# Wavelet convolution, batch norms and median blur on one core: the first stage's work is divided anew between POOL, VectorE and TensorE

## The chip, the cores and the metric

The kernel runs on one NeuronCore of a Trainium2 chip. The metric is the device time of one execution in microseconds. Data are float32 throughout; only the matmuls that do nothing but keep TensorE busy are bf16.

## What is computed

The input x has 16 images of 128 channels and 32 x 32 pixels. Cut to what matters:

```
a1, h1, v1, d1 = dwt2(x)                      # one Haar step over rows and columns: four 16x16 bands
proc(c)  = relu(batchnorm(einsum(c, conv_w)) * gamma + beta)   # 1x1 conv, statistics over all images
rimg0    = idwt2(proc(a1), proc(h1), proc(v1), proc(d1))
rimg1    = x                                   # three dwt steps and their inverses give x back
y        = conv3x3(concat([rimg0, rimg1]), convW_w) + convW_b
y        = relu(batchnorm(y))                  # statistics over all images again
out      = y + conv1x1(median3x3(y), W) + b
```

Both batch norms need a statistic over all 16 images before any image can go on. That divides the kernel into a first stage (split, 1x1 conv, bands, statistics), a long middle (3x3 conv and the medians of its output), and an end.

## The kernel before

Channels lie on the 128 partitions. All engines run programs written out by hand, in program order, and wait on semaphores. Nothing but these orders sets the order of the work.

**First stage, image by image.** SP's queue loads image n into one of eight ring buffers (`ring`; the program's names for them are raw, ru03, ru12 and xu03). `make_xu12` (L201, L202) adds and subtracts the even and odd columns and writes them to the image's slot in y. VectorE does this for the images in `BY_DVE` = (0, 5, 10) with `split_x`, POOL for the other 13. TensorE multiplies by w1 into one_ps, which has room for two images (`through_w1`, L332; four rows of the trace for an image, since an f32 matmul shows twice). ScalarE copies the odd rows out (`keep_odd`, L448), and VectorE adds and subtracts even and odd rows into the four bands in z (`bands`, L595 and L596). The product of image n+2 waits for the bands of image n. Then statistics: VectorE takes three bands with `band_stats` (L602), for two images at once, and `image_stats` (L607) for the last two images; ScalarE sums the fourth band and its squares.

**The taps.** The 3x3 conv is computed in a form that works on sums and differences of columns. For it the three column taps are mixed once: outer sum, middle plus outer, middle minus outer (`mix_taps`, L614 to L618, on VectorE behind the bands of image 2), and one half of them is halved by ScalarE (L472, L473).

**Early products.** The 3x3 conv works in units: an image, or half of one for images 0, 1, 14 and 15. The products of x for the first two units, `pq_of_x`, 12 of them, do not need the statistics. TensorE does them between the w1 products of images 5 to 13, as many behind each as `FILLS` says (L350, conv_ps<-y).

**After the statistics.** VectorE aggregates (L640), a short chain of tiny operations gives scale and shift, ScalarE normalises the bands of images 0 and 1 (`norm_bands`, L484), VectorE makes the row sums and differences of each (`make_ru12`, L208 and L209), and TensorE starts `pq_of_r` for units 0 and 1, four groups of three products, and then `outputs(0)`. POOL makes two more planes for every image (`make_xu03`, L269 and L271; `make_ru03`, L284 to L292). From then on VectorE alternates between `seed` (L688, L689) and the median network (L710 to L763).

**TensorE's clock.** `WARM_UP` matmuls on zeros stand at the start of the program (L393), and `KEEP_WARM` ones (L428) before the last stage.

Of the kernel before, what the change touches and what calls it, by code (L numbers as in the profile page):

```python
# [5 lines left out]
def wavelet_conv_median_kernel(nc, x, w1_t, w3_t, w2_t, vectors, out):  # L6
# [14 lines left out]
    PIX = H * W  # L21
# [14 lines left out]
    WARM_UP, KEEP_WARM = 8, 24  # L36
# [27 lines left out]
    with ctx:  # L64
# [75 lines left out]
        dve_done = sem("dve_done")  # L140
        taps_mixed = sem("taps_mixed")
# [5 lines left out]
        bands_normed = sem("bands_normed")  # L147
        ru12_made = sem("ru12_made")
# [99 lines left out]
        def _(pool):  # L248
# [6 lines left out]
            for n in BY_POOL:  # L255
                pool.wait_ge(x_in[n % RING], 16 * (n // RING + 1))
                make_xu12(G, n).then_inc(xu12_by_pool, 1)

# [64 lines left out]
        def _(pe):  # L323
# [71 lines left out]
            early = [(u, b, ky) for u in range(2) for b in range(2) for ky in KY_ORDER]  # L395
# [6 lines left out]
            assert not early  # L402
# [35 lines left out]
        def _(act):  # L438
# [28 lines left out]
            for n in range(IMAGES):  # L467
                keep_odd(n)
                if n == 3:
# [11 lines left out]
            def norm_bands(n):  # L481
                for b in range(BANDS):
                    band = zslot(n)[:, b * BAND:(b + 1) * BAND]
                    ins = S.activation(band, band, ACT.Relu, bias=bn1[:, 5, b:b + 1], scale=bn1[:, 4, b:b + 1])  # L484
                ins.then_inc(bands_normed, 1)
# [82 lines left out]
        def _(dve):  # L568
# [29 lines left out]
            def band_stats(p):  # L598
                dve.wait_ge(bands_made, 2 * p + 2)
                two = z[:, 2 * p:2 * p + 2, :].rearrange("c a q -> c (a q)")  # L600
                for b in range(DIAG):
                    step(V.bn_stats(stats1[:, b, p, :], at(two, b * BAND, [[PIX, 2], [1, BAND]])))  # L602
# [6 lines left out]
            def mix_taps():  # L609
                dve.wait_ge(w3_in, 16)  # L610
                row = [[KX * CH, 2 * KY], [1, CH]]
                left, mid, right = (at(wt[:, :], kx * CH, row) for kx in range(KX))
                dense = [[CH, 2 * KY], [1, CH]]
                step(V.tensor_tensor(at(outer_taps, 0, dense), left, right, ALU.add))  # L614
                after()
                step(V.tensor_tensor(at(v1[:, :], 0, dense), mid, at(outer_taps, 0, dense), ALU.add))
                after()
                V.tensor_tensor(mid, mid, at(outer_taps, 0, dense), ALU.subtract).then_inc(taps_mixed, 1)  # L618

            split_x(0)  # L620
            for n in range(IMAGES):
                bands(n)
                if n == 2:
                    mix_taps()
                if n == 3:
# [47 lines left out]

            for t in (col_lo, col_mid, col_hi):
                step(V.memset(at(t, 0, [[PITCH, H + 1]]), LOW))

            for n in range(2):
                dve.wait_ge(bands_normed, n + 1)
                wait_xu12(dve, RING + 5 - n)
                make_ru12(V, n).then_inc(ru12_made, 1)  # L680
# [209 lines left out]
```

## Time and profile before

| | before |
|---|---|
| median of 3 runs | 449.26 us (449.07 to 454.04) |
| profiled execution | 449.9 us, its span 447.8 us |
| TensorE busy | 403.3 us, 90% |
| VectorE busy | 408.8 us, 91% |
| ScalarE busy | 149.1 us, 33% |
| POOL busy | 197.9 us, 44% |
| mean granted TensorE clock | 0.96 of full speed |

Times in the trace count from the span's start. Two engines are busy nine tenths of the span, so shares alone do not tell which is waited for; the rows below are read from single stretches. The granted clock is given as a share of full speed: 1.00 is 2.4 GHz, 0.50 is 1.2 GHz.

### The profile page before, as it was taken

Reading aid. Unit: us, or ns where it says so; the run is one execution under the profiler, and the core shown is the slowest. Engines: PE = TensorE matmul, PEld = TensorE weight load, DVE = VectorE, ACT = ScalarE, POOL = GpSimd, SP = SyncE. Lnnn points to the kernel's source line nnn. Section 1 sums busy time; section 2 is a strip of 40 time slices with the busy share of each in tenths; the row PEclk is TensorE's granted clock in tenths of the full one; section 3 lists DMA queues with packets and bytes.
Section 4 is the critical chain, followed back from the end, with each engine's and each line's share of the span. In section 5 each row is a group of like instructions: output and inputs, shape, how many; then the busy total and the mean of one; then the engine's idle time right before and its main releaser. Section 6 shows DMA issues by size and latency. Waiting matters only on the chain.

```text
span 447.8 us, 3637 instructions
## 1 busy us (share of the span) xinstructions
PE 403.3 (90%) x1119; PEld 214.6 (48%) x1120; DVE 408.8 (91%) x535; ACT 149.1 (33%) x342; POOL 197.9 (44%) x186
## 2 busy tenths in 40 slices
PE   7497809999999999999999999999999986858896
PEld 2143408885544444444444444444446675743332
DVE  2978874799987999999999999999999999999996
ACT  2333663341413132223313132223313321216922
POOL 5996009080628182644627182644628510003730
PEclk9978967999999999999999999999999998969999
DMA  8960020010011010101011010101010000000557
GB/s 315 405 240 1 2 94 0 0 49 0 10 40 47 0 48 0 48 0 47 8 40 48 0 47 0 48 0 47 9 39 1 0 1 1 0 0 0 228 242 282
DMA packets 7651, 26.70 MB, mean 60 GB/s; under 512 B 976, under 2 KB 1232, under 8 KB 7504
## 3 DMA queue, kind: packets, MB, share of 16 engines
q1 hardware_dynamic: 7632, 26.48, 15.6%
q8 instruction: 8, 0.13, 0.1%
q14 instruction: 11, 0.09, 0.1%
HBM read 18.09 MB, written 8.39 MB: 59 GB/s over the span
## 4 chain that ended last, share of the span: by engine, by line
DVE 69%; PE 25%; issue 3%; ACT 1%; DMA 1%; POOL 0%; DVEq 0%; SPq 0%
PE conv_ps L350 19%; PE one_ps L332 5%; DVE one_ps L711 4%; DVE sorted_cols L747 4%; DVE one_ps L759 4%; DVE one_ps L761 4%; DVE sorted_cols L755 4%; DVE z L763 3%; DVE one_ps L745 3%; DVE sorted_cols L716 3%; DVE sorted_cols L714 3%; DVE sorted_cols L718 3%; DVE sorted_cols L713 3%; DVE sorted_cols L757 3%; DVE sorted_cols L753 3%; DVE y L841 3%
## 5 line engine op out<-in xcount | busy, mean ns | idle before, releaser
L350 PE MATMUL conv_ps<-ru,wt 128*128 128x512 f32 (+1 forms) x360 | 133.6, 508 | 0.0
L350 PE MATMUL conv_ps<-xu,wt 128*128 128x496 f32 (+3 forms) x240 | 89.9, 512 | 11.5 <-DVE conv_ps L689 11.5
L350 PEld LDWEIGHTS conv_ps<-ru,wt 128*128 128x128 f32 x360 | 70.5, 196 | 53.7 <-issue 49.7
L518 ACT ACTIVATE y<-conv_ps,sgn 128x512 f32<-128x512 f32 (+1 forms) x40 | 25.5, 639 | 185.1 <-PE conv_ps L350 185.1
L269 POOL TENSOR_TENSOR xu<-raw 128x480 f32<-128x480 f32 x16 | 17.2, 1072 | 139.5 <-PE conv_ps L350 139.4
L350 PEld LDWEIGHTS conv_ps<-xu,wt 128*128 128x128 f32 x240 | 46.6, 195 | 48.2 <-issue 33.2
L350 PE MATMUL conv_ps<-ru,v 128*128 128x496 f32 (+3 forms) x120 | 45.6, 518 | 12.7 <-DVE ru L209 12.7
L350 PE MATMUL conv_ps<-y,v 128*128 128x496 f32 (+3 forms) x120 | 44.6, 504 | 0.0
L350 PE MATMUL conv_ps<-y,wt 128*128 128x496 f32 (+3 forms) x120 | 44.2, 500 | 0.0
L332 PE MATMUL one_ps<-y,w 128*128 128x512 f32 x64 | 34.5, 669 | 10.7 <-DVE y L202 9.8
L350 PEld LDWEIGHTS conv_ps<-ru,v 128*128 128x128 f32 x120 | 24.0, 201 | 31.6 <-issue 16.6
L420 PE MATMUL conv_ps<-z,w 128*128 128x512 f32 x64 | 30.3, 613 | 4.0 <-DVE y L841 4.0
L484 ACT ACTIVATE z<-z,bn 128x256 f32<-128x256 f32 x64 | 33.0, 590 | 1.2 <-DVE bn L672 1.2
L284 POOL TENSOR_TENSOR eo<-ru 128x512 f32<-128x512 f32 x16 | 21.7, 1356 | 26.2 <-DVE ru L209 26.1
L350 PEld LDWEIGHTS conv_ps<-y,v 128*128 128x128 f32 x120 | 23.1, 192 | 20.3 <-issue 19.5
L350 PEld LDWEIGHTS conv_ps<-y,wt 128*128 128x128 f32 x120 | 22.9, 191 | 19.7 <-issue 18.9
L511 ACT ACTIVATE p_kept<-conv_ps 128x512 f32<-128x512 f32 (+1 forms) x20 | 10.3, 513 | 56.3 <-PE conv_ps L350 56.3
L524 ACT ACTIVATE conv_ps<-conv_ps,neg_shift,sgn 128x512 f32<-128x512 f32 (+1 forms) x40 | 26.3, 658 | 0.0
L332 PEld LDWEIGHTS one_ps<-y,w 128*128 128x128 f32 x64 | 13.0, 213 | 26.1 <-issue 11.6
L710 DVE TENSOR_TENSOR one_ps<-y 128x512 f32<-128x512 f32 (+2 forms) x20 | 14.9, 747 | 9.4 <-ACT y L518 8.8
L711 DVE TENSOR_TENSOR one_ps<-y 128x512 f32<-128x512 f32 (+2 forms) x20 | 22.7, 1135 | 0.0
L314 POOL MEMSET z<- 128x2 f32 x2 | 0.2, 102 | 49.4 <-ACT z L549 49.4
(120 smaller groups left out, 662.8 us busy)
## 6 DMA issues: line engine op xcount, KB each, us to landing
raw<-x SPq DMA_DIRECT2D x20, 512.0 KB, 3.3
out<-y SPq DMA_DIRECT2D x15, 512.0 KB, 2.6
ru<-x SPq DMA_DIRECT2D x8, 512.0 KB, 8.4
xu<-x SPq DMA_DIRECT2D x4, 512.0 KB, 7.8
wt<-w_t SPq DMA_DIRECT2D x1, 1152.0 KB, 8.4
out<-y SPq DMA_DIRECT2D x2, 256.0 KB, 2.8
w<-w_t SPq DMA_DIRECT2D x2, 64.0 KB, 3.8
vec<-vectors SPq DMA_DIRECT2D x1, 3.0 KB, 8.8
```

The source lines that it names most:

```text
L284: G.tensor_tensor(even, u1, u2, ALU.add)
L332: mm = nc.tensor.matmul(one_ps[:, n % 2, b * BANK:(b + 1) * BANK], w1[:, :], slot(n)[:, b * BANK:(b + 1) * BANK], start=True, stop=True)
L350: return nc.tensor.matmul(bank(u, b)[:, (r0 - row) * BW:(r1 - row) * BW], taps(half, kx, ky), plane[:, (r0 + dy) * BW:(r1 + dy) * BW], sta ...
L420: mm = nc.tensor.matmul(conv_ps[:, k, b * BANK:(b + 1) * BANK], w2[:, :], zslot(n)[:, b * BANK:(b + 1) * BANK], start=True, stop=True)
L484: ins = S.activation(band, band, ACT.Relu, bias=bn1[:, 5, b:b + 1], scale=bn1[:, 4, b:b + 1])
L518: S.activation(at(slot(n), row * W + b, [[2, cols]]), src, ACT.Identity, scale=sgn[:, :], accum_out=y_sum[:, part:part + 1]).then_inc(y_ke ...
L524: S.activation(src, src, ACT.Square, bias=neg_shift[:, :], scale=sgn[:, :], accum_out=y_sq[:, part:part + 1]).then_inc(squares_summed, 1)
L711: step(V.tensor_tensor(sorted_rows(HALF), even, odd, ALU.max))
L747: step(V.tensor_tensor(padded(col_lo), both(HALF), outer(col_hi), ALU.min))
L755: step(V.tensor_tensor(padded(col_hi), both(0), padded(col_hi), ALU.max))
L759: step(V.tensor_tensor(dense, dense, body(col_lo), ALU.max))
L761: step(V.tensor_tensor(dense, dense, body(col_hi), ALU.min))
```

## The change

- POOL splits all images but 0 and 2. VectorE splits those two before its first bands. The loads of the vectors and the taps stand behind the eight first images in SP's queue.
- The mixing of the taps moves from VectorE (behind image 2) to POOL (behind its last split). ScalarE halves behind image 15.
- The pair statistics are spread: two bands of a pair behind the bands of an even image, the third behind those of the next odd one.
- The 12 early products all stand behind the last w1 product. Behind them come 30 bf16 matmuls on zeros, the bridge, into one_ps.
- VectorE makes the row sums of image 0 in two parts, the first when two of its four bands are normalised, and TensorE's first group waits only for that part.

```
-    BY_DVE = (0, 5, 10)
+    BY_DVE = (0, 2)
-    LEAD = 5
-    FILLS = (1, 1, 1, 1, 1, 1, 2, 2, 2, 0, 0)
+    WARM_UP, KEEP_WARM, BRIDGE = 8, 24, 30
...
             for n in range(RING):
                 sp.dma_start(ring[n][:, :], x_img[:, n, :]).then_inc(x_in[n], 16)
-                if n == 3:
-                    sp.dma_start(wt[:, :], w3_cols).then_inc(w3_in, 16)
-                if n == 4:
-                    sp.dma_start(vec[:, :], vectors).then_inc(vec_in, 16)
+            sp.dma_start(vec[:, :], vectors).then_inc(vec_in, 16)
+            sp.dma_start(wt[:, :], w3_cols).then_inc(w3_in, 16)
...
                 make_xu12(G, n).then_inc(xu12_by_pool, 1)
+            pool.wait_ge(w3_in, 16)
+            G.tensor_tensor(at(outer_taps, 0, dense), left, right, ALU.add).then_inc(outer_summed, 1)
+            pool.wait_ge(outer_summed, 1)
+            G.tensor_tensor(at(v1[:, :], 0, dense), mid, at(outer_taps, 0, dense), ALU.add).then_inc(v1_mixed, 1)
+            pool.wait_ge(v1_mixed, 1)
+            G.tensor_tensor(mid, mid, at(outer_taps, 0, dense), ALU.subtract).then_inc(taps_mixed, 1)
...
             for n in range(IMAGES):
                 through_w1(n)
-                if n == LEAD:
-                    pe.wait_ge(taps_halved, 2)
-                for _ in range(FILLS[n - LEAD] if n >= LEAD else 0):
-                    pq_of_x(*early.pop(0))
+            pe.wait_ge(taps_halved, 2)
+            for u in range(2):
+                for b in range(2):
+                    for ky in KY_ORDER:
+                        pq_of_x(u, b, ky)
+            pe.wait_ge(bands_made, IMAGES - 1)
+            for _ in range(BRIDGE):
+                nc.tensor.matmul(one_ps[:, 0, 0:BANK], zeros[:, 0:CH], zeros[:, :], start=True, stop=True)
+            pe.wait_ge(first_sums_made, 1)
+            pq_of_r(0, 0, p_done)
             pe.wait_ge(ru12_made, 1)
-            for u in range(2):
-                for b, done in enumerate((p_done, q_done)):
-                    pq_of_r(u, b, done)
+            pq_of_r(0, 1, q_done)
+            for b, done in enumerate((p_done, q_done)):
+                pq_of_r(1, b, done)
...
                 keep_odd(n)
-                if n == 3:
+                if n == IMAGES - 1:
                     act.wait_ge(taps_mixed, 1)
...
-            split_x(0)
+            for n in BY_DVE:
+                split_x(n)
             for n in range(IMAGES):
                 bands(n)
-                if n == 2:
-                    mix_taps()
-                if n + 2 in BY_DVE:
-                    split_x(n + 2)
+                if n >= 2 and n % 2 == 0:
+                    pair_stats(n // 2 - 1, 0)
+                    pair_stats(n // 2 - 1, 1)
                 if n >= 3 and n % 2:
-                    band_stats((n - 3) // 2)
+                    pair_stats((n - 3) // 2, 2)
...
+            for k, (normed, made) in enumerate(((first_pair_normed, first_sums_made), (bands_normed, ru12_made))):
+                dve.wait_ge(normed, 1)
+                upper, lower = (at(zslot(0), k * HALF + b * BAND, [[BW, BH], [1, BW]]) for b in range(2))
+                rows = ru12[0][:, k * HALF:(k + 1) * HALF]
+                V.tensor_tensor(at(rows, 0, [[2 * BW, BH], [1, BW]]), upper, lower, ALU.add)
+                V.tensor_tensor(at(rows, BW, [[2 * BW, BH], [1, BW]]), upper, lower, ALU.subtract).then_inc(made, 1)
```

VectorE, from the bands of image 1 to the statistics behind image 3, before: z is the bands, sorted_cols and v and wt the taps being mixed, y<-ru_0 the split of image 5.

```order
L595 TENSOR_TENSOR z<-one_ps,sorted_cols 128x2x256
L596 TENSOR_TENSOR z<-one_ps,sorted_cols 128x2x256
L614 TENSOR_TENSOR sorted_cols<-wt 128x768
L616 TENSOR_TENSOR v<-wt,sorted_cols 128x768
L618 TENSOR_TENSOR wt<-wt,sorted_cols 128x6x128
L595 TENSOR_TENSOR z<-one_ps,sorted_cols 128x2x256
L596 TENSOR_TENSOR z<-one_ps,sorted_cols 128x2x256
L579 TENSOR_SCALAR sgn<-vec 128x1
L628 TENSOR_SCALAR sgn<-sgn 128x1
L629 TENSOR_SCALAR half_bn<-vec 128x1
L630 TENSOR_SCALAR half_bn<-vec 128x1
L201 TENSOR_TENSOR y<-ru_0 128x512
```

VectorE, the same place now, from the bands of image 2 on.

```order
L610 TENSOR_TENSOR z<-one_ps,sorted_cols 128x2x256
L611 TENSOR_TENSOR z<-one_ps,sorted_cols 128x2x256
L616 BN_STATS stats<-z 128x6 x2
L610 TENSOR_TENSOR z<-one_ps,sorted_cols 128x2x256
L611 TENSOR_TENSOR z<-one_ps,sorted_cols 128x2x256
L616 BN_STATS stats<-z 128x6
```

The mixing and the split are gone from between the bands, and the statistics come as two and one.

TensorE, from the last w1 products to the first products of r, before: one_ps<-y is w1, conv_ps<-y an early product, conv_ps<-ru_0 a product of r.

```order
L332 MATMUL one_ps<-y,w 128x512 x2
L350 MATMUL conv_ps<-y,v 128x240
L350 MATMUL conv_ps<-y,wt 128x256
L332 MATMUL one_ps<-y,w 128x512 x2
L350 MATMUL conv_ps<-y,wt 128x256
L350 MATMUL conv_ps<-y,wt 128x240
L332 MATMUL one_ps<-y,w 128x512 x4
L350 MATMUL conv_ps<-ru_0,v 128x256
```

TensorE, the same place now.

```order
L341 MATMUL one_ps<-y,w 128x512 x32
L359 MATMUL conv_ps<-y,v 128x256
L359 MATMUL conv_ps<-y,v 128x240
L359 MATMUL conv_ps<-y,v 128x256
L359 MATMUL conv_ps<-y,wt 128x256
L359 MATMUL conv_ps<-y,wt 128x240
L359 MATMUL conv_ps<-y,wt 128x256
L359 MATMUL conv_ps<-y,v 128x256 x2
L359 MATMUL conv_ps<-y,v 128x240
L359 MATMUL conv_ps<-y,wt 128x256 x2
L359 MATMUL conv_ps<-y,wt 128x240
L413 MATMUL one_ps<-zeros 128x512 x30
```

The early products that stood between w1 products now stand behind the last of them, and the bridge stands between them and the products of r.

POOL, from its last split to its planes of x, now; before, the planes (L269, L271) followed the last split directly.

```order
L202 TENSOR_TENSOR y<-xu_0 128x512
L262 TENSOR_TENSOR sorted_cols<-wt 128x768
L264 TENSOR_TENSOR v<-wt,sorted_cols 128x768
L266 TENSOR_TENSOR wt<-wt,sorted_cols 128x6x128
L278 TENSOR_TENSOR xu_0<-raw 128x32x15
```

The three operations on the taps stand between.

## Rows read from the trace of the kernel before

**Rows 1.** The chain that ended last, in order of time: start us, us, what

```profile
66.80 69.06 PE conv_ps L350 x240
137.57 1.39 DVE one_ps L711
```

**Rows 2.** VectorE's timeline: start us, us, engine, line, out<-in, count, idle before and releaser

```profile
8.70 0.69 DVE L595 TENSOR_TENSOR z<-one_ps,sorted_cols 128x512 f32<-128x512 f32 x1 [2.77 <-ACT sorted_cols L448]
...
14.15 1.49 DVE L614 TENSOR_TENSOR sorted_cols<-wt 128x768 f32<-128x768 f32 x1
...
18.99 0.68 DVE L595 TENSOR_TENSOR z<-one_ps,sorted_cols 128x512 f32<-128x512 f32 x1
...
54.78 0.69 DVE L595 TENSOR_TENSOR z<-one_ps,sorted_cols 128x512 f32<-128x512 f32 x1
...
55.99 1.87 DVE L602 BATCH_NORM_STATS2 stats<-z 128x6 f32<-128x512 f32 x3
57.77 2.04 DVE L607 BATCH_NORM_STATS2 stats<-z 128x6 f32<-128x256 f32 x6
59.85 0.40 DVE L640 BATCH_NORM_AGGREGATE mv<-stats 128x2 f32<-128x54 f32 x1
...
65.45 0.69 DVE L208 TENSOR_TENSOR ru<-z 128x512 f32<-128x512 f32 x1 [1.97 <-ACT z L484]
```

**Rows 3.** POOL's timeline, the same columns

```profile
6.21 1.04 POOL L201 TENSOR_TENSOR y<-raw 128x512 f32<-128x512 f32 x1 [4.78 <-DMA raw<-x]
7.21 1.04 POOL L202 TENSOR_TENSOR y<-raw 128x512 f32<-128x512 f32 x1
...
12.79 1.04 POOL L201 TENSOR_TENSOR y<-ru 128x512 f32<-128x512 f32 x1 [0.55 <-DMA ru<-x]
...
16.50 1.75 POOL L202 TENSOR_TENSOR y<-xu 128x512 f32<-128x512 f32 x1
...
34.79 1.04 POOL L202 TENSOR_TENSOR y<-xu 128x512 f32<-128x512 f32 x1
...
66.82 1.26 POOL L284 TENSOR_TENSOR eo<-ru 128x512 f32<-128x512 f32 x1 [26.05 <-DVE ru L209]
...
71.17 1.04 POOL L292 TENSOR_TENSOR ru<-eo 128x512 f32<-128x512 f32 x1
```

**Rows 4.** TensorE's timeline, the same columns

```profile
8.30 6.04 PE L332 MATMUL one_ps<-y,w 128*128 128x512 f32 x12 [0.26 <-POOL y L202]
...
23.01 3.78 PE L332 MATMUL one_ps<-y,w 128*128 128x512 f32 x4 [6.15 <-DVE y L202]
...
39.01 3.55 PE L332 MATMUL one_ps<-y,w 128*128 128x512 f32 x4 [2.31 <-DVE y L202]
...
50.52 3.60 PE L332 MATMUL one_ps<-y,w 128*128 128x512 f32 x8
...
74.98 1.43 PE L350 MATMUL conv_ps<-xu,wt 128*128 128x256 f32 x6
76.25 1.43 PE L350 MATMUL conv_ps<-ru,wt 128*128 128x256 f32 x6
...
404.12 5.13 PE L428 MATMUL conv_ps<-zeros 128*128 128x512 bf16 x23
```

**Rows 5.** Stretches of one microsecond, TensorE: length, busy (count), granted clock, DMA share, GB/s

```profile
38.00:39.00 1.00, 0.00 (x0) 0.90 0.03 8
...
72.00:73.00 1.00, 1.00 (x4) 0.54 0.00 0
```

**Rows 6.** ScalarE's timeline

```profile
19.53 0.51 ACT L473 ACTIVATE wt<-wt 128x384 f32<-128x384 f32 x1
...
54.16 0.60 ACT L448 ACTIVATE sorted_cols<-one_ps 128x512 f32<-128x512 f32 x1 [1.12 <-PE one_ps L332]
...
58.06 0.18 ACT L460 ACTIVATION_READ_ACCUMULATOR sorted_cols<-z,diag_neg_shift 128x1 f32 x1
...
63.34 4.04 ACT L484 ACTIVATE z<-z,bn 128x256 f32<-128x256 f32 x8 [1.19 <-DVE bn L672]
```

More of the change, by code:

```diff
@@ L35, in wavelet_conv_median_kernel @@
     R_HALF, X_HALF = 0, 1
-    WARM_UP, KEEP_WARM = 8, 24
+    WARM_UP, KEEP_WARM, BRIDGE = 8, 24, 30
     RING = 8
-    BY_DVE = (0, 5, 10)
+    BY_DVE = (0, 2)
     BY_POOL = tuple(n for n in range(IMAGES) if n not in BY_DVE)
-    LEAD = 5
-    FILLS = (1, 1, 1, 1, 1, 1, 2, 2, 2, 0, 0)
     BN3_AT, FINISH_AT = 9, (19, 20, 22, 24, 25, 27, 28, 30, 31, 32, 34, 35)
@@ L140, in wavelet_conv_median_kernel @@
         dve_done = sem("dve_done")
+        outer_summed = sem("outer_summed")
+        v1_mixed = sem("v1_mixed")
         taps_mixed = sem("taps_mixed")
@@ L147, in wavelet_conv_median_kernel @@
         bands_normed = sem("bands_normed")
+        first_pair_normed = sem("first_pair_normed")
+        first_sums_made = sem("first_sums_made")
         ru12_made = sem("ru12_made")
@@ L257, in _ @@
                 make_xu12(G, n).then_inc(xu12_by_pool, 1)
+            pool.wait_ge(w3_in, 16)
+            row = [[KX * CH, 2 * KY], [1, CH]]
+            left, mid, right = (at(wt[:, :], kx * CH, row) for kx in range(KX))
+            dense = [[CH, 2 * KY], [1, CH]]
+            G.tensor_tensor(at(outer_taps, 0, dense), left, right, ALU.add).then_inc(outer_summed, 1)
[3 more added lines that the diff above has]
+            G.tensor_tensor(mid, mid, at(outer_taps, 0, dense), ALU.subtract).then_inc(taps_mixed, 1)
             def make_xu03(n):
@@ L394, in _ @@
             pe.wait_ge(w1_halved, 1)
-            early = [(u, b, ky) for u in range(2) for b in range(2) for ky in KY_ORDER]
             for n in range(IMAGES):
                 through_w1(n)
-                if n == LEAD:
-                    pe.wait_ge(taps_halved, 2)
-                for _ in range(FILLS[n - LEAD] if n >= LEAD else 0):
-                    pq_of_x(*early.pop(0))
-            assert not early
+            pe.wait_ge(taps_halved, 2)
[8 more added lines that the diff above has]
+            pq_of_r(0, 0, p_done)
             pe.wait_ge(ru12_made, 1)
-            for u in range(2):
-                for b, done in enumerate((p_done, q_done)):
-                    pq_of_r(u, b, done)
+            pq_of_r(0, 1, q_done)
+            for b, done in enumerate((p_done, q_done)):
+                pq_of_r(1, b, done)
             for u in range(2, len(UNITS) + 1):
@@ L484, in norm_bands @@
                     ins = S.activation(band, band, ACT.Relu, bias=bn1[:, 5, b:b + 1], scale=bn1[:, 4, b:b + 1])
+                    if n == 0 and b == 1:
+                        ins.then_inc(first_pair_normed, 1)
                 ins.then_inc(bands_normed, 1)
@@ L596, in bands, with pair_stats @@
                 V.tensor_tensor(at(zslot(n), BAND, [[HALF, 2], [BW, BH], [1, BW]]), even, odd, ALU.subtract).then_inc(bands_made, 1)
-            def band_stats(p):
+            def pair_stats(p, b):
                 dve.wait_ge(bands_made, 2 * p + 2)
                 two = z[:, 2 * p:2 * p + 2, :].rearrange("c a q -> c (a q)")
-                for b in range(DIAG):
-                    step(V.bn_stats(stats1[:, b, p, :], at(two, b * BAND, [[PIX, 2], [1, BAND]])))
+                step(V.bn_stats(stats1[:, b, p, :], at(two, b * BAND, [[PIX, 2], [1, BAND]])))
             def image_stats(n, group):
@@ L607, in image_stats @@
                     step(V.bn_stats(stats1[:, b, group, :], z[:, n, b * BAND:(b + 1) * BAND]))
[L609 to L618, printed above, removed]
-            split_x(0)
+            for n in BY_DVE:
+                split_x(n)
             for n in range(IMAGES):
                 bands(n)
-                if n == 2:
-                    mix_taps()
-                if n == 3:
+                if n == 6:
                     dve.wait_ge(vec_in, 16)
@@ L672, in _ @@
             V.tensor_scalar(shift1, t, -1.0, half_bn1[:, 1:2], ALU.mult, ALU.add).then_inc(bn1_ready, 1)
+            dve.wait_ge(taps_mixed, 1)
             for t in (col_lo, col_mid, col_hi):
@@ L677, in _ @@
             for n in range(2):
-                dve.wait_ge(bands_normed, n + 1)
                 wait_xu12(dve, RING + 5 - n)
-                make_ru12(V, n).then_inc(ru12_made, 1)
+            for k, (normed, made) in enumerate(((first_pair_normed, first_sums_made), (bands_normed, ru12_made))):
[4 more added lines that the diff above has]
+                V.tensor_tensor(at(rows, BW, [[2 * BW, BH], [1, BW]]), upper, lower, ALU.subtract).then_inc(made, 1)
+            dve.wait_ge(bands_normed, 2)
+            make_ru12(V, 1).then_inc(ru12_made, 1)
             def seed(u):
```

## The prediction

> **What bounds the kernel now.** I read the chain of work that ended last first, in order of time. Its longest piece is a single run of TensorE from 66.80 to 135.86 us (240 rows), and from 137.6 on it is VectorE's median network to the end [rows 1]. So nothing after 66.80 waits for anything but TensorE's own products and, behind them, VectorE, which itself waited for TensorE's first outputs. What counts is when TensorE begins that run and at what clock. The first stage is therefore worth its full price at the end: there is no slack between 66.80 and 447.8 that could swallow an earlier start.
>
> Then I read the first stage engine by engine. VectorE makes the bands of image 0 at 8.70 and reaches the aggregation of the statistics at 59.85 [rows 2], 51.2 us later. Its unit prices: two band operations 1.20 (54.78 to 55.99), the three statistics of a pair 1.78, the six of the last two images 2.08, the mixing of the taps 4.84 (14.15 to 18.99) [rows 2]. Bands and statistics need 16 x 1.20 + 7 x 1.78 + 2.08 = 33.7. The other 17.5 us of the 51.2 are the mixing (4.8), two splits of x in the middle of the stage, and waits. The waits come from order: image 5 and image 10 are split by VectorE behind other work, so TensorE stood idle 6.15 us until 23.01 and 2.31 until 39.01 [rows 4]. The second of these pauses took the granted clock from 1.00 to 0.50 (0.90 in the microsecond from 38 on) [rows 5], and one image's product then took 3.55 where two take 3.60 at full clock (50.52) [rows 4]; from one start to the next that is 3.4 against 1.71, the tail of the last row taken off. TensorE also sits idle 12.7 (from 54.12 on) before 66.80 and starts there at half clock: in the microsecond from 72 on the mean is still 0.54 [rows 5]. This cold start makes the way from 66.80 to the first outputs 8.2 us long (74.98), where its four groups take 5.1 warm; 3.1 are the clock's.
>
> **The change, part by part.** *Splits to POOL.* VectorE splits only images 0 and 2, ahead of its first bands; POOL has the other 14. POOL's two operations for an image take 2.00 us start to start (6.21, 7.21) and the same late in the stage, while VectorE makes bands and statistics (34.79) [rows 3]. The transfers of the taps and vectors go behind the eight images: POOL waited 0.55 for image 4 [rows 3], behind the taps' transfer, and should not now. With 0.5 for the moment after image 1, when image 3 has to be there and VectorE's split of image 2 runs alongside, POOL has image 15 at 6.2 + 0.5 + 14 x 2.0 = 34.7.
>
> *VectorE.* It begins the bands at 9.2 (8.70 plus half a microsecond of the second split that nothing hides; 8.7 and 10.2 are the ends). A pair of images costs it 4.18 (2.40 + 1.78), POOL 4.00, TensorE 3.42, and the round through a PSUM bank (product 1.9, ScalarE's copy 0.6, bands 1.3, handovers) 3.9 for two images. So VectorE is the bound once statistics flow. Spreading them between bands removes no work; it keeps 1.8 us blocks from standing between two products. Before image 4 VectorE has 1.2 to do per image and gets one per 2.0, which costs 1.5 of idleness. With 0.4 for the sign and halves it reaches the aggregation at 9.2 + 33.7 + 0.4 + 1.5 = 44.8 against 59.85: 15.0 earlier.
>
> *The mixing on POOL* is three operations of 768 columns. POOL never did that size here; by columns they are 1.5 x 1.00 each, 4.6 together with two waits (4.5 to 7.7 if each ran as the slowest 512-column row did, 1.75 [rows 3]). From 34.7 it ends at 39.3. ScalarE needs it behind the copy of image 15. The bands of image 15 start at 44.8 - 2.08 - 0.6 - 1.2 = 41.0; those of image 13 end at 38.0, the last product runs 38.1 to 40.0, ScalarE copies until 40.6. So POOL is early by 1.3, and ScalarE's two halvings (0.94, by 19.53 and its 0.51 [rows 6]) end at 41.6. ScalarE's remaining sums and squares (3.6, as from 54.65, where its last copy lets go, to 58.24 [rows 6]) end at 45.2, with VectorE's aggregation, and the table load behind them lies beside VectorE's little chain. POOL's shifted differences of x, which stand behind the mixing in its queue, are due only after 58.
>
> *Early products and bridge.* TensorE has finished w1 at 40.0, waits 1.6 for the halves, then runs the 12 early products, which used to fill the gaps: 3 take 1.27 (74.98 to 76.25 [rows 4]), 12 take 5.1, to 46.7. The bridge is 30 products of 512 bf16 columns; 23 took 5.13 at full clock [rows 4], 0.218 apart, so 30 take 6.6, to 53.3. The statistics' road is shorter: 59.85 to 63.34 before [rows 2, 6] makes 48.3 for the first normalisation, two of image 0's four bands 1.1, the first half sums on VectorE 0.8 (two of half the columns of the 0.69 at 65.45 [rows 2], with a handover): 50.2. So **the bridge, not the sums, ends last**, by 3.1 us, and TensorE begins the run at 53.3, warm.
>
> *The sum.* From there four groups of three products (4 x 1.27 = 5.1) lead to the first outputs at 58.4; before, they began at 74.98 [rows 4]. POOL's last planes for them, 5.4 us behind the sums (66.82 to 71.17 and one operation more [rows 3]), are there at 56.5. All that follows repeats the old order and durations: 74.98 - 58.4 = 16.6 us. Of these 13.5 are the earlier start, and 3.1 the clock. The profiled run took 449.9, 447.8 of it span; that gives 433.3. The median of the three runs is 0.6 lower, and I take **433.0**.
>
> *Clock at the gap.* The uncertain term is the 1.6 us gap before the early products. An idle of 2.31 took the clock away, one of 0.26 did not [rows 4]. If it falls, five of the twelve products run at half clock, about 2.5 us more: 435.5.
>
> *A rule against the change.* POOL's operations are 1.00 apart where VectorE's of the same 512 columns are 0.60 apart [rows 2, 3], 1.66 times. The Trainium skill's page GPSIMD Engine Reference, section 4.1 Engine selection, says to put elementwise work on VectorE, since POOL is about 2 times slower with two inputs. An estimate with that factor puts POOL's operations 1.2 apart and the time at about 438. The row is this kernel's own, and it keeps the sum at 433; what decides is that POOL has the time, which the rule does not ask.
>
> **Rivals.**
> *POOL becomes the bound (slower).* Beside VectorE's mixing a POOL operation took 1.75 instead of 1.04 [rows 3]. If VectorE's new neighbours, bands and statistics, slow it as much, its 28 operations and the mixing, 32.6 us, grow by the factor 1.7 to 55.4: 22.8 more, of which 1.3 are covered. TensorE's run then starts 21.5 later than forecast, 433.3 + 21.5 = 454.8, slower than before. It costs from a factor of 1.04 on and turns the change into a loss from 1.55. Against it: the row at 34.79 has 1.04 in the middle of VectorE's bands and statistics, as the one at 7.21 has with VectorE idle. Behind it, the page SBUF — State Buffer, section Who interferes with whom: VectorE contends with POOL's reads when both of its inputs lie in SBUF. The mixing and the splits are such, the bands, with one input in PSUM, are not; the trace agrees (1.75 against 1.04), and by the rule the price stays 433. Chance 0.04.
> *The clock falls within the first stage.* Without fills TensorE works 1.71 of every 2.1 us. If that does not keep 1.00, each product costs 3.4. From image 5 (16.8) eleven of them end at 54.2, the halves at 55.9. Six us of dense work at half clock and the rest at full end the early products at 64.1, the bridge at 70.7, and the outputs start at 75.8: 450.7. Against it: from 8.30 on TensorE took 6.04 for three images, 2.01 each, without fills, and the clock stayed [rows 4]. Chance 0.05.
> *The stage packs worse than reckoned.* VectorE and POOL differ by only 4% a pair, ScalarE's and TensorE's handovers lie between, and waits that I count once may come for every pair. 0.3 us for each of 8 pairs and a later first band make 3 to 5 us: 436 to 439. Chance 0.13.
> *The bridge does not bind.* If the early products start sooner or the sums come later than 53.3, it costs nothing; at best 3.1 less than forecast, 430. Chance 0.08.
> *The gain is given back later.* The median network could have been late for another reason. The chain runs through TensorE until 135.9 and only then to VectorE [rows 1], so both move together. Chance 0.02, about 445.
>
> **How the numbers follow.** The forecast has 0.43 with a clock that stays, and 0.25 with one that falls at the gap. 433.0 is the likeliest. The range of 8 in 10 takes both, the bridge that does not bind, and most of a worse packing: 429.5 to 438.5. Two per cent (about what a measurement of this kernel can tell from no change) is 9 us, so faster means below 440.3: 0.89. The fall within the stage and a mild form of POOL's slowness lie within 2%: 0.08. Slower than 458.2 takes POOL at more than 1.7 and a cold start besides: 0.03.
>
> **What would show it.** Aggregation near 44.8; POOL's mixing done before ScalarE's last copy; the early products in one piece from 41.6; 30 bf16 products between them and the first r products; VectorE's first half sums about 3 us before the bridge ends; granted clock 1.00 from the bridge on; first outputs near 58.4; and the rest of the trace shifted as a block. I am wrong if POOL's operations are longer than 1.04 beside the bands, if TensorE's image products are 3.4 us, or if the run of TensorE after the bridge shows new gaps that the old one did not have.

## The result, and the profile after

The changed kernel takes 434.12 us (median of 4 runs, 433.21 to 434.62), against 449.5 for the kernel before (4 runs): a ratio of 0.963, 95% interval 0.957 to 0.970. The profiled execution, the fastest of the four, took 433.21; its span is 431.4, 16.4 less than the 447.8 before, with a mean granted clock of 0.99.

VectorE's timeline of the changed kernel, the rows that answer to [rows 2]:

```profile
9.29 0.68 DVE L610 TENSOR_TENSOR z<-one_ps,sorted_cols 128x512 f32<-128x512 f32 x1
...
13.33 0.69 DVE L610 TENSOR_TENSOR z<-one_ps,sorted_cols 128x512 f32<-128x512 f32 x1 [1.12 <-ACT sorted_cols L461]
...
15.73 0.67 DVE L610 TENSOR_TENSOR z<-one_ps,sorted_cols 128x512 f32<-128x512 f32 x1
...
16.92 0.68 DVE L616 BATCH_NORM_STATS2 stats<-z 128x6 f32<-128x512 f32 x1
...
42.91 2.04 DVE L621 BATCH_NORM_STATS2 stats<-z 128x6 f32<-128x256 f32 x6
44.98 0.40 DVE L644 BATCH_NORM_AGGREGATE mv<-stats 128x2 f32<-128x54 f32 x1
...
50.20 0.42 DVE L691 TENSOR_TENSOR ru<-z 128x256 f32<-128x256 f32 x1
```

The bands start at 9.29, 0.6 us later than before, and between the second wait for ScalarE (until 13.33) and the aggregation at 44.98 VectorE is never idle; before, the aggregation was reached at 59.85. The first half sums (the sums and differences of two of image 0's four bands) are done at 50.62.

POOL's timeline, for [rows 3]:

```profile
9.34 1.04 POOL L201 TENSOR_TENSOR y<-ru 128x512 f32<-128x512 f32 x1 [1.12 <-DMA ru<-x]
...
34.27 1.06 POOL L202 TENSOR_TENSOR y<-xu 128x512 f32<-128x512 f32 x1
35.26 1.84 POOL L262 TENSOR_TENSOR sorted_cols<-wt 128x768 f32<-128x768 f32 x1
...
39.08 1.81 POOL L266 TENSOR_TENSOR wt<-wt,sorted_cols 128x768 f32<-128x768 f32 x1
...
51.59 1.27 POOL L293 TENSOR_TENSOR eo<-ru 128x512 f32<-128x512 f32 x1 [6.86 <-DVE ru L691]
```

The splits start 1.00 apart beside bands and statistics all the way, 1.04 to 1.06 each. The mixing, though, takes 1.81 to 1.84 per operation and ends at 40.9.

ScalarE, its last copy and the first halving:

```profile
40.36 0.60 ACT L461 ACTIVATE sorted_cols<-one_ps 128x512 f32<-128x512 f32 x1 [1.77 <-PE one_ps L341]
40.92 0.52 ACT L485 ACTIVATE v<-v 128x384 f32<-128x384 f32 x1
```

TensorE, for [rows 4]:

```profile
34.20 3.74 PE L341 MATMUL one_ps<-y,w 128*128 128x512 f32 x8 [0.42 <-DVE z L611]
38.37 1.95 PE L341 MATMUL one_ps<-y,w 128*128 128x512 f32 x4 [0.43 <-DVE z L611]
41.91 1.54 PE L359 MATMUL conv_ps<-y,v 128*128 128x256 f32 x6 [1.59 <-ACT wt L486]
...
47.09 6.64 PE L413 MATMUL one_ps<-zeros 128*128 128x512 bf16 x30
53.57 1.43 PE L359 MATMUL conv_ps<-ru,v 128*128 128x256 f32 x6
...
58.64 1.43 PE L359 MATMUL conv_ps<-xu,wt 128*128 128x256 f32 x6
```

Before, TensorE paused 6.15 and 2.31 us within the stage; now the pauses are 0.4 to 0.8 for each pair of images, and 1.59 before the early products. These run in one piece, the bridge behind them ends 2.9 us after the half sums are ready (50.62), and the products of r start warm (at full clock) at 53.57. The first outputs start at 58.64, 74.98 before.

The longest piece of the chain that ended last, for [rows 1]:

```profile
53.73 65.79 PE conv_ps L359 x240
```

The run of 240 rows is 65.79 long where it was 69.06. (The chain counts it here from the end of the bridge, 0.16 after its first row at 53.57.) Together with its start it ends 16.3 us earlier, and VectorE's median network begins its first full image at 120.45 against 136.78, 16.33 earlier: the span's 16.4 are all made before that point.

One part of the change brought nothing here: the row sums of image 0 in two parts. With the 6.9 us that lay between the aggregation and the whole sums before (59.85 to 66.75), sums in one piece would have been ready at about 51.9 (an estimate), and the bridge ends at 53.6. No run tries that part alone.

### The profile page after: what moved, and what is told of

Its sections match the earlier page's. It is cut to its first block, busy times and chain, and to the rows that moved or that the text cites. A ratio compares the mean times of both kernels' runs of the same rounds, so it can differ in the third digit from the quotient of the medians.

```text
span 431.4 us, 3699 instructions
## 1 busy us (share of the span) xinstructions
PE 403.5 (94%) x1150; PEld 212.9 (49%) x1150; DVE 400.2 (93%) x532; ACT 148.7 (34%) x342; POOL 201.6 (47%) x191
## 4 chain that ended last, share of the span: by engine, by line
DVE 71%; PE 23%; issue 3%; DMA 1%; ACT 0%; SPq 0%; DVEq 0%
PE conv_ps L359 19%; DVE one_ps L724 4%; DVE sorted_cols L760 4%; DVE one_ps L772 4%; DVE one_ps L774 4%; DVE sorted_cols L768 4%; DVE one_ps L758 4%; DVE z L776 4%; DVE sorted_cols L729 4%; DVE sorted_cols L727 4%; DVE sorted_cols L731 4%; DVE sorted_cols L726 4%; DVE sorted_cols L770 3%; DVE sorted_cols L766 3%; DVE y L854 3%
## 5 line engine op out<-in xcount | busy, mean ns | idle before, releaser
L359 PE MATMUL conv_ps<-ru,v 128*128 128x496 f32 (+3 forms) x120 | 43.7, 500 | 0.0
L341 PE MATMUL one_ps<-y,w 128*128 128x512 f32 x64 | 30.2, 610 | 5.3 <-DVE z L611 3.8
L359 PEld LDWEIGHTS conv_ps<-y,v 128*128 128x128 f32 x120 | 22.7, 190 | 20.0 <-issue 16.6
L359 PEld LDWEIGHTS conv_ps<-ru,v 128*128 128x128 f32 x120 | 22.8, 190 | 17.7 <-issue 16.6
L359 PEld LDWEIGHTS conv_ps<-y,wt 128*128 128x128 f32 x120 | 22.8, 190 | 17.6 <-issue 16.6
L539 ACT ACTIVATE conv_ps<-conv_ps,neg_shift,sgn 128x512 f32<-128x512 f32 (+1 forms) x40 | 26.4, 660 | 0.0
L341 PEld LDWEIGHTS one_ps<-y,w 128*128 128x128 f32 x64 | 10.9, 189 | 24.7 <-issue 17.8
```

Of the source, the lines that this page charges most:

```text
L341: mm = nc.tensor.matmul(one_ps[:, n % 2, b * BANK:(b + 1) * BANK], w1[:, :], slot(n)[:, b * BANK:(b + 1) * BANK], start=True, stop=True)
L359: return nc.tensor.matmul(bank(u, b)[:, (r0 - row) * BW:(r1 - row) * BW], taps(half, kx, ky), plane[:, (r0 + dy) * BW:(r1 + dy) * BW], sta ...
L539: S.activation(src, src, ACT.Square, bias=neg_shift[:, :], scale=sgn[:, :], accum_out=y_sq[:, part:part + 1]).then_inc(squares_summed, 1)
```

## The experiments

Eleven kernels were run beside the changed one. Each was timed against the kernel before (medians of 4 runs, of 10 for before_bridge), not against the changed kernel; the medians of the kernel before lie between 449.5 and 450.4 in all sessions. Span, aggregation and start of the r products are those of one profiled execution. The last column is when VectorE's median network begins its first full image.

This column compares kernels better than the span does: from there to the end it takes 310.9 to 312.1 us in every execution, and the difference does not go with the edit. bridge15 and x_half_first both stand at 117.44, and their spans differ by 1.1.

| kernel | median us (range) | ratio to before, 95% | span | aggregation | r products from | first full image |
|---|---|---|---|---|---|---|
| changed | 434.12 (433.2 to 434.6) | 0.963 (0.957 to 0.970) | 431.4 | 44.98 | 53.57 | 120.45 |
| bridge15 | 431.59 (430.3 to 432.8) | 0.960 (0.956 to 0.963) | 428.4 | 44.78 | 50.40 | 117.44 |
| bridge0 | 434.16 (433.7 to 434.8) | 0.965 (0.961 to 0.969) | 432.9 | 46.39 | 52.09 | 121.91 |
| mix_on_dve | 440.26 (440.1 to 441.9) | 0.980 (0.976 to 0.983) | 438.3 | 51.82 | 60.31 | 127.19 |
| stats_lumped | 435.14 (434.9 to 435.9) | 0.968 (0.965 to 0.971) | 433.0 | 46.60 | 54.03 | 120.92 |
| dve_0_5_10 | 440.11 (438.4 to 444.3) | 0.982 (0.974 to 0.990) | 436.6 | 49.92 | 58.42 | 125.30 |
| pool_15 | 435.78 (434.5 to 437.7) | 0.969 (0.964 to 0.975) | 433.8 | 44.41 | 55.64 | 122.52 |
| before_bridge | 446.36 (443.4 to 449.9) | 0.990 (0.985 to 0.995) | 445.1 | 60.14 | 67.09 | 134.07 |
| fills_back | 440.65 (438.8 to 441.1) | 0.978 (0.971 to 0.984) | 439.2 | 55.27 | 60.79 | 127.82 |
| split_only | 443.18 (442.6 to 445.2) | 0.985 (0.978 to 0.991) | 440.6 | 52.72 | 59.66 | 129.62 |
| x_half_bridge15 | 431.79 (431.2 to 432.5) | 0.959 (0.952 to 0.967) | 429.4 | 45.35 | 50.96 | 118.00 |
| x_half_first | 431.42 (430.2 to 433.2) | 0.958 (0.952 to 0.965) | 429.5 | 44.68 | 50.40 | 117.44 |

**Is the bridge the last to end?** Half of it:

```
-    WARM_UP, KEEP_WARM, BRIDGE = 8, 24, 30
+    WARM_UP, KEEP_WARM, BRIDGE = 8, 24, 15
```

> The changed kernel with 15 bridge matmuls in place of 30. Theory A (the bridge ends last before the products of r): the early products still end near 47.1, the bridge near 50.4, the first half sums are made near 50.6, so TensorE's run starts at 50.7 instead of 53.6 with the clock still at 1.00; span 431.4 - 2.9 = 428.5, or up to 0.5 more if POOL's planes of r (ready near 57.0) hold the first outputs. Rival B (the end is set by VectorE's or POOL's way behind the statistics, the bridge only lies beside it): span unchanged at 431.4 within 0.5.

TensorE's timeline of bridge15:

```profile
46.81 3.40 PE L413 MATMUL one_ps<-zeros 128*128 128x512 bf16 x15
50.40 1.54 PE L359 MATMUL conv_ps<-ru,v 128*128 128x256 f32 x6 [0.19 <-DVE ru L691]
```

The 15 matmuls end at 50.21, VectorE's half sums at 50.34, and the products start at 50.40 (their idle time of 0.19 names the half sums), 3.17 earlier than in the changed kernel. Of that, 0.28 is the stage itself, whose sums came at 50.34 instead of 50.62. Span 428.4, 3.0 less, as theory A had it. The bridge had been on the path with its last 13 matmuls; rival B falls. The medians say the same more weakly: 431.59 against 434.12, ranges apart, but the two ratios' intervals overlap.

**Is the bridge needed at all?** None of it (`BRIDGE` = 0):

> The changed kernel without any bridge matmul. TensorE is idle from 47.1 to about 50.7, 3.6 us. Theory A1 (the clock falls in such a pause and the run starts cold): granted clock 0.50 for some 6 us from 50.7 on, about 3 us lost, first outputs near 58.6 and span near 431.5, so the 30 bridge matmuls of the changed kernel bought nothing net. Theory A2 (3.6 us is still bridged by nothing): clock stays, span 428.5, like 15 matmuls. Rival B (the bridge lies beside something longer and only keeps the clock): span 431.4 + 3 = 434.5.

TensorE's timeline of bridge0, then stretches of one microsecond (length, busy, granted clock, DMA share, GB/s):

```profile
52.09 2.85 PE L359 MATMUL conv_ps<-ru,v 128*128 128x256 f32 x6 [3.51 <-DVE ru L691]
54.73 2.71 PE L359 MATMUL conv_ps<-ru,wt 128*128 128x256 f32 x6
```

```profile
51.00:52.00 1.00, 0.00 (x0) 0.52 1.02 410
...
57.00:58.00 1.00, 1.00 (x5) 0.57 0.00 0
```

The pause is 3.51 us, the clock falls to 0.50 and comes back in the microsecond from 57 on. Three products take 2.64 to the next start where they take 1.27 warm, and the run of 240 rows is 68.88 long from its first row, nearly as long as before the change (69.06), against 66.11 in bridge15. That is theory A1, and it gives 2.8 us for the cold start. The median equals the changed kernel's (434.16 and 434.12): 30 bf16 matmuls cost what they bring, 15 cost nothing. In this execution the whole first stage also ran 1.4 us later than in the changed kernel (the aggregation at 46.39), from the first image products on, so the spans, 432.9 against 431.4, do not compare alone; the lengths of the run do.

**The clock's share alone, in the kernel before.** The edit, and the rows of TensorE's timeline:

```
             assert not early
+            pe.wait_ge(bands_made, IMAGES - 1)
+            for _ in range(52):
+                nc.tensor.matmul(one_ps[:, 0, 0:BANK], zeros[:, 0:CH], zeros[:, :], start=True, stop=True)
```

> The kernel before with 52 bf16 matmuls on zeros behind its last w1 product and nothing else changed: they fill TensorE's pause from 54.7 to about 66.3. Theory A (the cold start at 66.80 costs 3.1 us at the end): granted clock 1.00 from 66.8 on, first outputs near 71.9 instead of 74.98, span 444.7. Rival H (the first products wait for POOL's planes and VectorE's sums anyway, at 72.2 and later, so that a warm TensorE waits): span 447 to 448.

```profile
55.12 11.40 PE L405 MATMUL one_ps<-zeros 128*128 128x512 bf16 x52 [0.72 <-DVE z L599]
67.09 1.53 PE L350 MATMUL conv_ps<-ru,v 128*128 128x256 f32 x6 [0.57 <-DVE ru L209]
...
72.27 1.43 PE L350 MATMUL conv_ps<-xu,wt 128*128 128x256 f32 x6
```

The first outputs stand at 72.27, 5.18 behind the start where it was 8.18; the run of 240 rows takes 66.05, and the span is 445.1. The ratio is 0.990 (0.985 to 0.995). This is theory A, and nothing else was late at 72. The first full image starts 2.71 earlier, a little under 3.0 because this execution reached the aggregation 0.3 later.

**Is VectorE's work the bound of the stage?** The mixing put back on VectorE, and the loads of taps and vectors back between those of the images:

```
             for n in range(IMAGES):
                 bands(n)
+                if n == 2:
+                    mix_taps()
...
```

> The changed kernel with the mixing of the taps put back on VectorE behind the bands of image 2, and the loads of taps and vectors back between the images; ScalarE halves behind image 15 as in the changed kernel. Theory A (VectorE's sum of work sets the end of the statistics): mixing costs VectorE 4.8, of which at most 1 falls into waits it has anyway; aggregation at 49 to 50 instead of 45.0, span 435.4 to 436.4. Rival C (POOL's 14 splits pace the stage and VectorE has room): aggregation within 1.5 of 45.0, span 431 to 433.

VectorE's timeline of mix_on_dve, TensorE's, then POOL's:

```profile
14.30 0.69 DVE L602 TENSOR_TENSOR z<-one_ps,sorted_cols 128x512 f32<-128x512 f32 x1 [1.05 <-ACT sorted_cols L453]
```

```profile
22.46 5.37 PE L333 MATMUL one_ps<-y,w 128*128 128x512 f32 x8 [4.73 <-DVE z L603]
28.10 3.79 PE L333 MATMUL one_ps<-y,w 128*128 128x512 f32 x8 [0.26 <-DVE z L603]
```

```profile
13.66 1.04 POOL L201 TENSOR_TENSOR y<-ru 128x512 f32<-128x512 f32 x1 [1.99 <-DMA ru<-x]
...
15.65 1.76 POOL L201 TENSOR_TENSOR y<-ru 128x512 f32<-128x512 f32 x1
```

Aggregation at 51.82, span 438.3: 6.8 and 6.9 more, beyond the 4.8 of the operations and beyond the range that I gave. Of the 6.8, 1.0 has nothing to do with the mixing: the bands of image 2, ahead of it, already start at 14.30 where the changed kernel had 13.33. That leaves 5.9. The rest beyond 4.8 is seen above. The taps' transfer is again in front of image 4, for which POOL waits 1.99; POOL's splits take 1.75 beside the mixing; TensorE pauses 4.73, loses the clock, and takes 5.37 for two images that take 3.74 warm. The loads and the mixing were moved together, so their shares are not separated. Rival C falls: VectorE has no room for the mixing.

**Blocks of statistics:** all three of a pair behind the odd image.

```
                 if n >= 3 and n % 2:
+                    for b in range(DIAG):
+                        pair_stats((n - 3) // 2, b)
```

> The changed kernel with the three pair statistics again in one block behind each odd image. Theory A (only the sum of VectorE's work counts, since the round through the PSUM banks fits beside the block): a wait of about 0.1 per pair, aggregation at 45.0 to 46.0, span 431.4 to 432.4. Rival D (the blocks of 1.8 us stand between products and cost a wait for every pair): 1 us or more in each of 7 pairs, aggregation at 52 or later, span 438 or more.

VectorE's timeline of stats_lumped:

```profile
41.54 0.69 DVE L610 TENSOR_TENSOR z<-one_ps,sorted_cols 128x512 f32<-128x512 f32 x1 [0.32 <-ACT sorted_cols L461]
...
42.74 1.87 DVE L616 BATCH_NORM_STATS2 stats<-z 128x6 f32<-128x512 f32 x3
44.53 2.04 DVE L621 BATCH_NORM_STATS2 stats<-z 128x6 f32<-128x256 f32 x6
```

A wait of 0.32 stands before the second image of the pair shown, and the last pair's block lies wholly behind the last bands. Aggregation at 46.60, 1.6 later, above the 45 to 46 that I expected, far below rival D. The bridge hides all but 0.46 of it (53.57 to 54.03), and the first full image starts 0.47 later. The median is 1.0 above the changed kernel's, with intervals that overlap; whether spreading is worth 0.5 or 1 us behind this bridge these runs don't settle. With the short bridge it should be worth more, since the half sums came 1.5 us later (52.08 against 50.62); that was not run.

**The two splits in mid-stage:** `BY_DVE = (0, 5, 10)`, split two images ahead, all else changed.

> The changed kernel with VectorE splitting images 0, 5 and 10 at the places where the kernel before did it, all else as changed. Theory A (VectorE is the bound, and a split in the middle is work plus a product that comes late): two mid-stage splits of 1.3 to 2.4 each less the one at the start, 1.3 to 3.5 net, plus a late product at each; aggregation at 46.5 to 49.5, span 433 to 436. Rival E (the pauses of 6.15 and 2.31 with their falls of the clock come from these splits alone and return): granted clock at 0.50 twice in the stage, aggregation at 50 or later, span 437 or more.

TensorE's timeline of dve_0_5_10, then its clock in the longer pause:

```profile
19.61 3.84 PE L341 MATMUL one_ps<-y,w 128*128 128x512 f32 x8 [2.94 <-DVE y L202]
...
32.48 1.98 PE L341 MATMUL one_ps<-y,w 128*128 128x512 f32 x4 [2.12 <-DVE y L202]
```

```profile
18.00:19.00 1.00, 0.00 (x0) 1.00 1.02 418
19.00:20.00 1.00, 0.39 (x1) 1.00 1.05 430
```

Aggregation at 49.92, 4.9 later, span 436.6. The pauses are back (2.94 and 2.12), but the clock stays at 1.00 in this execution: a half of rival E is true, and its half on the clock is not. My upper bounds for theory A, 49.5 and 436, were 0.4 and 0.6 short. The profiled execution is the fastest of the four; the others have spans of 437.7, 438.9 and 442.5, all in rival E's range, the last with a mean granted clock of 0.967 against 0.984 here. They have no trace, so whether the clock fell in their pauses is open.

**The same part alone, in the kernel before:**

```
-    BY_DVE = (0, 5, 10)
+    BY_DVE = (0, 2)
-            split_x(0)
+            for n in BY_DVE:
+                split_x(n)
...
-                if n + 2 in BY_DVE:
-                    split_x(n + 2)
```

> The kernel before with one part of the change alone: VectorE splits images 0 and 2 ahead of its bands, POOL all others; mixing, blocks of statistics, early products and no bridge as before. Theory A (the parts of the change add up by VectorE's work and TensorE's clock): the change without this part lost 5.0 in span (dve_0_5_10 against the changed kernel), so this part alone should bring about 4 to 7: aggregation at 53 to 56 instead of 59.85, a cold run from 60 to 63, span 441 to 444. Rival (the part is worth something only together with the mixing on POOL, since VectorE's mixing stops TensorE anyway): span 446 or more.

TensorE's and VectorE's timelines of split_only:

```profile
20.48 2.91 PE L332 MATMUL one_ps<-y,w 128*128 128x512 f32 x4 [3.55 <-DVE z L596]
```

```profile
52.72 0.40 DVE L639 BATCH_NORM_AGGREGATE mv<-stats 128x2 f32<-128x54 f32 x1
```

Aggregation at 52.72, 7.1 earlier than before, cold run from 59.66, span 440.6. In spans it is worth 7.2 alone and 5.2 as the last part, by the first full image 7.2 and 4.9; the mixing, which still stops TensorE for 3.55 here, does not take it away. Theory A's range, 4 to 7, is missed by 0.2 on the good side; the rival falls.

**The early products between the w1 products again** (with the mixing on VectorE, which they need, ScalarE's halving behind image 3 and a bridge of 48):

```
                 through_w1(n)
...
+                if n == 5:
+                    pe.wait_ge(taps_halved, 2)
+                for _ in range((1, 1, 1, 1, 1, 1, 2, 2, 2, 0, 0)[n - 5] if n >= 5 else 0):
+                    pq_of_x(*early.pop(0))
```

> The kernel with the mixing on VectorE (mix_on_dve) and, besides, ScalarE's halving behind image 3 and the 12 early products again between the w1 products of images 5 to 13, with 48 bridge matmuls. Compared with mix_on_dve (aggregation 51.8, run from 60.3, span 438.3). Theory A (VectorE's work sets the end of the statistics, the fills cost TensorE time that it has, and the early products in one piece behind the last w1 product are what makes the bridge end late): aggregation 51.8 to 53.5 (three images with two fills each cost TensorE 5.1 a pair against VectorE's 4.2), run from about 57.5 to 59.5 right behind the sums, span 435.5 to 437.5. Rival (the fills themselves delay the w1 products much): aggregation at 55 or later, span 439 or more.

Aggregation at 55.27, 3.45 later than in mix_on_dve, span 439.2 against 438.3. That is the rival's number, but not all of it comes from the fills. VectorE's timeline of fills_back, then TensorE's:

```profile
14.71 0.69 DVE L603 TENSOR_TENSOR z<-one_ps,sorted_cols 128x512 f32<-128x512 f32 x1 [0.88 <-ACT sorted_cols L454]
```

```profile
23.70 3.73 PE L333 MATMUL one_ps<-y,w 128*128 128x512 f32 x4 [5.60 <-DVE z L604]
...
41.35 1.88 PE L333 MATMUL one_ps<-y,w 128*128 128x512 f32 x4
...
43.90 1.88 PE L333 MATMUL one_ps<-y,w 128*128 128x512 f32 x4
...
50.35 10.53 PE L406 MATMUL one_ps<-zeros 128*128 128x512 bf16 x48 [0.29 <-DVE z L604]
60.79 1.54 PE L351 MATMUL conv_ps<-ru,v 128*128 128x256 f32 x6
```

The w1 product of image 5 starts at 23.70 (22.46 in mix_on_dve), 1.24 later, and no fill stands before it: image 2's bands began 0.41 later (14.71, 14.30), and the first operation of VectorE's mixing took 1.83 where it took 1.00. The fills' share is what follows. From there to the end of the last w1 product it is 26.4 against 24.7, since images with two fills behind them are 2.55 apart (41.35, 43.90), more than VectorE's 2.1, and to the aggregation 31.6 against 29.4. So fills do delay the images, by 2.2 us; without the 1.24 the aggregation would stand at 54.0 (an estimate), between theory A's 53.5 and the rival's 55.

The median is 440.65 against 440.26, so at the end both orders cost the same, but the long bridge of mix_on_dve is part of that. There the half sums were made at 57.37 and the run waited for the 30 matmuls until 60.31; here they were made at 60.74, and the run starts at 60.79. With a bridge cut to fit, the order in one piece should be about 3 us ahead, an estimate from these times that was not run.

**POOL's margin.** One more split on POOL (`BY_DVE = (0,)`):

> The changed kernel with POOL splitting 15 images and VectorE only image 0. POOL's mixing ended at 40.9 in the changed kernel, just when ScalarE could use it. Theory F (POOL has no margin left): POOL's last split ends near 36.2, the mixing near 41.8, the halves near 42.7, early products and bridge 0.9 later, run from 54.4, and TensorE's pause before the early products is 2.5 instead of 1.6. If the clock survives that: span 432.3. If it falls as after the 2.31 of the kernel before: about 2.5 more, 434.8. Rival G (POOL had the 1.3 us of margin that was forecast): span unchanged at 431.4 within 0.3.

TensorE's timeline of pool_15 and its clock:

```profile
42.53 2.88 PE L359 MATMUL conv_ps<-y,v 128*128 128x256 f32 x6 [2.78 <-ACT wt L486]
45.19 1.60 PE L359 MATMUL conv_ps<-y,wt 128*128 128x256 f32 x6
...
55.64 1.43 PE L359 MATMUL conv_ps<-ru,v 128*128 128x256 f32 x6
```

```profile
41.00:42.00 1.00, 0.00 (x0) 1.00 0.00 0
42.00:43.00 1.00, 0.47 (x1) 0.55 0.00 0
```

The pause grows from 1.59 to 2.78, the clock falls, the first three products take 2.66 (42.53 to 45.19) to the next start, and the run begins 2.07 later, at 55.64; span 433.8. Theory F with the falling clock, 1 us less than its 434.8: the twelve early products take 6.63 where they took 5.18, so the fall costs 1.45 and not 2.5. VectorE itself was earlier (44.41), but then waited 1.20 for ScalarE's sums, which stand behind the halving. So POOL had no margin, and a bridge behind a late start makes it worse, since it ends last.

**Giving POOL margin.** The x half of the taps is mixed first, with 15 bridge matmuls (x_half_first: and POOL splits 15 images):

```
+            for k, half in enumerate((X_HALF, R_HALF)):
+                left, mid, right = (at(wt[:, :], (half * KY * KX + kx) * CH, row) for kx in range(KX))
...
```

> bridge15 with POOL mixing the x half of the taps first (three operations of 384 columns, then three for the other half), so that ScalarE can halve sooner. If an operation's time goes by its columns (1.81 for 768), three of 384 take 2.8 and end at 38.1, ScalarE halves right behind its last copy, as now, and all else stays: span as bridge15, 428.4 within 0.5. If three operations of 384 columns cost as much as three of 768 (a fixed price), the halves come no sooner and the six together end at 46.5, before the run: span 428.4 to 429.

> x_half_bridge15 with POOL splitting 15 images. In pool_15 the mixing ended at about 41.8 and came too late; here the x half ends near 39 and ScalarE halves right behind its last copy, near 41.2. VectorE starts its bands at 8.7 instead of 9.3. Theory A (VectorE's work is the bound): aggregation at 44.4, sums at 50.1, clock at 1.00 throughout, run from 50.1, span 428.1, 0.3 better than bridge15. Rival F (POOL is the bound already with 15 images): aggregation or halves later than in the changed kernel, span 429.5 or more.

POOL's timeline of x_half_first:

```profile
36.18 1.02 POOL L264 TENSOR_TENSOR sorted_cols<-wt 128x384 f32<-128x384 f32 x1
...
38.36 1.01 POOL L268 TENSOR_TENSOR wt<-wt,sorted_cols 128x384 f32<-128x384 f32 x1
...
41.48 1.01 POOL L268 TENSOR_TENSOR wt<-wt,sorted_cols 128x384 f32<-128x384 f32 x1
```

Six operations of 384 columns take 1.00 to 1.02 each, 6.3 together, so neither columns alone nor a fixed price sets them. The x half is ready at 39.4 with 15 splits, the clock stays, and the run starts at 50.40. Medians 431.79 and 431.42: the same as bridge15's 431.59 within the ranges. The spans, 429.4 and 429.5, are above what I expected (428.4 and 428.1), and for x_half_first in rival F's range, but not by rival F: its run and its first full image stand where bridge15's do, and the 1.1 us more fall behind that point. In x_half_bridge15 the stage itself ran 0.6 later (aggregation at 45.35). POOL's margin was gained and nothing came of it, because VectorE stays the bound and one split less saves it little: its bands start at 8.92 instead of 9.29, and the aggregation comes at 44.68 instead of 44.98 (44.78 in bridge15). The best time is thus about 431.5, by 15 bridge matmuls alone.

## Why the prediction was right

It gave 433.0 (429.5 to 438.5) and the measured median is 434.12. Step by step:

- **The chain decides, nothing later swallows the gain.** Right: the first full image of the median network moved by 16.33, the span by 16.4.
- **VectorE's sum.** 44.8 was reckoned for the aggregation, 44.98 measured. mix_on_dve and dve_0_5_10 show that this work is the bound, and that a sum of durations is only its lower part: putting back 4.8 cost 5.9 (6.8 less the 1.0 that stood before it), putting back two splits cost 4.9, because TensorE's and POOL's pauses come along. That 44.98 is so near is partly the luck of the execution profiled: in bridge0, whose program is the same up to that point, the aggregation came at 46.39, 1.4 us later.
- **POOL's splits.** 1.00 apart, as [rows 3] had them; ready at 35.3, not 34.7, since image 3's transfer kept POOL 1.12 where I had 0.5.
- **The mixing on POOL: mis-sized.** 4.6 was reckoned by columns, 5.6 measured (35.26 to 40.85); it lay within the bounds of 4.5 to 7.7, but I took the end nearest to the row of 1.04. With the 0.6 above, the margin of 1.3 was gone: the mixing ended at 40.9, and ScalarE's halving began at 40.92, right then. It cost 0.06, by luck; pool_15 shows what the next microsecond costs.
- **Early products and bridge.** Halves at 41.86 (41.6 reckoned), early products to 47.09 (46.7), run from 53.57 (53.3), half sums at 50.62 (50.2). That the bridge ends last, 2.9 us behind the sums, is shown by bridge15. It was reckoned at 3.1.
- **The clock.** It held through the pause of 1.59. The cold start's price, 3.1, is shown twice, a little smaller: 3.0 to the first outputs in before_bridge, 2.8 in the length of bridge0's run against bridge15's. The price of a fall at the gap, 2.5, was mis-sized, but no term of the sum: pool_15 shows 1.45, for about three of the twelve products at half clock and not five.
- **The rivals.** POOL at 1.75 was not seen beside bands and statistics, only beside operations with two inputs in SBUF (1.75 beside the mixing in mix_on_dve, 1.72 at 52.82 beside the row sums of the changed kernel), as both the row and the Trainium skill's page SBUF — State Buffer, section Who interferes with whom, have it. In the changed kernel the clock never fell within the stage; it fell where a pause was long, in mix_on_dve and before the early products of pool_15. A stage that packs worse did not come: VectorE waited 1.5 us for ScalarE, the 1.5 reckoned.
- **Not seen:** that the early products, taken out from between the images, speed the images up. I had put them down as a cost only, moved behind the stage. fills_back shows that they delay it, by 2.2 us there, with the mixing on VectorE; how much of the 15 us gained before the aggregation is theirs was not measured.

The sum was made for a profiled execution and gave 433.3, and the profiled one took 433.21: its first outputs came 0.2 later than reckoned (58.64, 58.4), and its span fell by 16.4 instead of 16.6. The median of the four is 0.9 above it, and 433.0 was taken 0.3 below the sum: that is the 1.1 us between forecast and median, less than the executions scatter (433.21 to 434.62).

## What to carry to other kernels

When a stage feeds a long saturated rest, find the step whose start is the rest's start and make the sum engine by engine up to it. Here each microsecond there was worth one at the end, and misplaced work cost more than its duration, because it stopped the engines that feed and follow it. Matmuls on zeros that keep the clock are free only up to the moment at which their successor's input is ready: count them against that moment, here 15 and not 30. An engine that takes over work and has "a microsecond of margin" by a price scaled from another shape has none; measure that shape first.

## What was not expected of the hardware

- The length of TensorE's pause did not tell by itself whether the clock would fall. It held through 2.94 and 2.12 us in dve_0_5_10 and 1.59 in the changed kernel, and fell with 2.31 in the kernel before [rows 4, 5], 2.78 in pool_15, and 3.51 in bridge0, each in one profiled execution. TensorE had been working on products at 1.00 before each of them; no run here separates what makes the difference.
- A POOL addition of f32 takes 1.04 to 1.06 us for 512 columns, 1.00 to 1.02 for 384 in rows of 128, 1.81 to 1.84 for 768 in rows of 128, and 1.27 for 512 in rows of 16 (51.59). The time follows columns within a layout only: 768 cost 1.8 times 384, and 384 of the taps as much as 512 of x. The cause was not tried.
- At the start of the program matmuls can run at half rate while the granted clock reads 1.00. The first image's took 1.06 to 1.19 us each in bridge0 and 0.59 to 0.70 in the changed kernel, with 1.00 in the rows of both, and the instructions up to there are the same. This is the 1.4 us by which bridge0's stage ran late; why it comes in some executions is open.
